# Two-layer graph block on one core: the row minimum of negated, scaled scores becomes the bias of the exponentials, with all engine orders rewritten

## The reference

```python
# layer 0
mi, mj = x @ Wi.T, x @ Wj.T
out = deg[None, :, None] * (mi + b) + einsum('ij,bjo->bio', a, mj)
x = layernorm(x + out)
# layer 1: 8 heads of 64
q, k, v = h @ Wq.T + bq, h @ Wk.T + bk, h @ Wv.T + bv
scores = einsum('bhqd,bhkd->bhqk', q, k) / sqrt(64)
scores = where(adj == 0, -inf, scores)
out = softmax(scores) @ v
x = layernorm(x + (out @ Wo.T + bo))
```

## Time and profile before

| | |
|---|---|
| Median of 3 runs | 3001.79 us (3000.93 to 3002.13) |
| The profiled execution's own time | 3026.84 us |
| Its span, first to last instruction | 3024.9 us |
| PE busy | 96% of the span |
| DVE busy | 79% |
| POOL busy | 62% |
| ACT busy | 62% |
| Share of the 16 DMA engines | 31% |
| Mean granted TensorE clock | 0.995 of full speed |

### The profile page before, as it was taken

The page is one execution under the profiler, slowest core; times in us unless marked ns, Lnnn a source line. Parts: engine busy times, 40 slices in busy tenths (PEclk is TensorE's granted clock), DMA queues, the critical chain, the costliest instruction groups (busy, mean ns, idle before and its releaser), DMA issues.

```text
span 3024.9 us, 59823 instructions
## 1 busy us (share of the span) xinstructions
PE 2903.7 (96%) x18584; PEld 2456.9 (81%) x18584; DVE 2377.9 (79%) x6029; ACT 1862.6 (62%) x4874; POOL 1877.5 (62%) x1793
## 2 busy tenths in 40 slices
PE   7999999999999999999999999999999999999997
PEld 5888888888788888888887888888888878878886
DVE  7787787877877878878778778787787787787876
ACT  4666656656666566666666665665666666656664
POOL 4666666666566666666665665666666666656563
PEclk9999999999999999999999999999999999999998
DMA  4333333333323333323333233332332332332321
GB/s 137 101 105 98 111 97 104 104 97 104 100 95 111 97 104 110 98 97 108 100 104 99 95 111 97 100 108 97 104 104 95 106 104 97 111 97 97 105 92 55
DMA packets 282404, 306.71 MB, mean 101 GB/s; under 512 B 18816, under 2 KB 214912, under 8 KB 282368
## 3 DMA queue, kind: packets, MB, share of 16 engines
q1 hardware_dynamic: 282368, 306.26, 31.2%
HBM read 173.55 MB, written 132.64 MB: 101 GB/s over the span
## 4 chain that ended last, share of the span: by engine, by line
PE 46%; DVE 24%; issue 16%; POOL 8%; ACT 5%; DVEq 1%; POOLq 0%; DMA 0%; SPq 0%; ACTq 0%
PE proj L493 25%; PE av L493 7%; PE proj L611 6%; DVE probs L1036 5%; PE attn L655 4%; ACT probs L820 4%; PE proj L530 3%; DVE oT L1087 3%; DVE exp_bias L1043 3%; DVE xb L1113 2%; POOL pT_lo L397 2%; DVE xb L1119 2%; PE attn L670 1%; DVE v_both L990 1%; POOL probs L388 1%
## 5 line engine op out<-in xcount | busy, mean ns | idle before, releaser
L820 ACT ACTIVATE probs<-probs,exp_bias 128x256 f32<-128x256 f32 x1024 | 508.6, 498 | 342.2 <-DVE exp_bias L1043 342.1
L388 POOL TENSOR_TENSOR probs<-probs,row_inv 128x512 f32<-128x512 f32 x256 | 266.5, 1041 | 476.6 <-DVE row_inv L1053 476.6
L1036 DVE CUSTOM_DVE_ANT_0 probs<-attn,mask_add 128x256 f32<-128x256 f32 x1024 | 381.1, 419 | 148.0 <-PE attn L655 147.7
L397 POOL TENSOR_TENSOR pT_lo<-pT_raw,pT_hi 128x512 fp32r<-128x512 f32 x315 | 402.9, 1296 | 149.2 <-ACT pT_hi L851 148.9
L530 PE MATMUL proj<-wji_hi,xs_hi 128*128 128x512 f32 x896 | 382.3, 427 | 24.7 <-DVE xb L1113 11.8
L530 PE MATMUL proj<-wji_hi,xs_lo 128*128 128x512 f32 x896 | 355.4, 397 | 0.0
L530 PE MATMUL proj<-wji_lo,xs_hi 128*128 128x512 f32 x896 | 355.3, 397 | 0.0
L611 PE MATMUL proj<-mj_hi,wq_hi 128*128 128x256 f32 x1024 | 293.5, 287 | 26.3 <-DVE mj_lo L990 26.3
L493 PE MATMUL av<-pT_hi,v_both 128*128 128x256 f32 x1016 | 266.1, 294 | 47.3 <-DVE oT L1087 29.1
L1144 DVE TENSOR_SCALAR hb<-hb,mean_var_out,rstd_out 128x512 f32<-128x512 f32 x128 | 122.3, 996 | 226.9 <-POOL rstd_out L415 226.9
L420 POOL TENSOR_TENSOR oT_lo<-oT,oT_hi 128x256 fp32r<-128x256 f32 x256 | 194.4, 759 | 151.7 <-ACT oT_hi L864 151.6
(11 more groups left out here) (125 smaller groups left out, 8824.5 us busy)
## 6 DMA issues: line engine op xcount, KB each, us to landing
bounce<-probs SPq DMA_DIRECT2D x189, 512.0 KB, 2.6
pT_raw<-bounce SPq DMA_DIRECT2D x756, 128.0 KB, 3.1
xs_raw<-in_xT SPq DMA_DIRECT2D x64, 512.0 KB, 4.1
xb<-in_x SPq DMA_DIRECT2D x64, 512.0 KB, 3.4
out<-hb SPq DMA_DIRECT2D x64, 512.0 KB, 2.8
w_raw<-in_w0T SPq DMA_DIRECT2D x8, 256.0 KB, 6.0
stage<-in_wqT SPq DMA_DIRECT2D x1, 1024.0 KB, 9.8
stage<-in_wkT SPq DMA_DIRECT2D x1, 1024.0 KB, 11.6
```

The costliest lines, as they stand in the source:

```text
L388: pool.tensor_tensor(e, e, inv, ALU.mult).then_inc(norm_odd_done, 1)
L397: pool.tensor_tensor(pT_lo[:, g % 2, :, :, i, :, :], pT_raw[:, g % 2, :, :, i, :, :], pT_hi[:, :, :, i, :, :].bitcast(F32), ALU.subtract). ...
L820: last = nc.scalar.activation(e, e, ACT.Exp, bias=exp_bias[:, g % 2, s:s + 1], scale=SCALE, accum_out=row_sum[:, g % 2, s:s + 1])
L1036: last = V.tensor_tensor_reduce(out=out_, in0=in_, in1=mask_, scale=1.0, scalar=MASKED, op0=ALU.add, op1=ALU.max, accum_out=row_max[:, g % ...
```

## The change

The weights and the bias of q are multiplied by -1/8 once, at the start: Wq's high part in ACT's copy, its raw values on POOL (half 0, in place, a new instruction with a wait behind it) and in DVE's subtraction (half 1), and `bq_cols` on DVE (128x4), for which ACT waits. So the scores come out negated and scaled. The mask is 0 or +3.0e38, the reduction is a minimum that starts from 1.0e37, and `row_min` is itself the bias: exp(row_min - e). `bias_of_pair`, `exp_bias` and `bias_done` are gone; the exponentials wait for the two minima of the pair. In `last_step` nothing else changes. In `step` the lists of POOL, PE, ACT and DVE are reordered; SP's is not.

```diff
-MASKED = -3.0e38
-MAX_FLOOR = -1.0e37
+MASKED = 3.0e38
+MIN_CEILING = 1.0e37
...
# POOL
             def sum_x(n):
+                pool.wait_ge(normed["h"], R * n)
                 pool.wait_ge(xT_loaded, 16 * (n + 1))
...
             pool.wait_ge(w_hi_done, 1)
+            pool.tensor_scalar(stage[0][:, 0:2, :], stage[0][:, 0:2, :], -SCALE, None, ALU.mult).then_inc(wq_scaled, 1)
+            pool.wait_ge(wq_scaled, 1)
...
                 n = b + 1
+                if y_: split_o(b - 1, 3)
                 normalise_odd(b, 1)
                 normalise_odd(b, 0)
-                if y_: split_o(b - 1, 3)
                 mj_low(n, 0)
                 mj_low(n, 1)
+                normalise_odd(b, 2)
                 root("h", n)
-                normalise_odd(b, 2)
-                if ahead: sum_x(b + 2)
                 p_low(b, 1, 0)
                 p_low(b, 1, 1)
                 normalise_odd(b, 3)
-                if ahead: add_bias(b + 2, parity)
-                split_o(b, 0)
+                if ahead: sum_x(b + 2)
                 p_low(b, 2, 0)
                 p_low(b, 2, 1)
+                if ahead: add_bias(b + 2, parity)
+                if y_: root("out", b - 1)
                 if ahead: x_low(b + 2, 0)
+                p_low(b, 3, 0)
+                if ahead: x_low(b + 2, 1)
+                split_o(b, 0)
                 split_o(b, 1)
-                if y_: root("out", b - 1)
-                p_low(b, 3, 0)
                 split_o(b, 2)
-                if ahead: x_low(b + 2, 1)
                 residual(n, 1 - parity, stored=y_)
...
# PE
                 attend(b, 0, not y_)
                 transpose_h(n, 0, 1 - parity)
+                scores(b, 1, only=3)
                 transpose_h(n, 1, 1 - parity)
-                scores(b, 1, only=3)
                 q(n, 0)
+                q(n, 1)
                 attend(b, 1)
-                q(n, 1)
                 k(n, 0)
                 k(n, 1)
+                v(n, 0)
                 attend(b, 2)
-                v(n, 0)
                 v(n, 1)
                 attend(b, 3)
...
# ACT
-                act.wait_ge(bias_done, G * b + at(g, tail) + 1)
+                act.wait_ge(max_done, 2 * (G * b + at(g, tail)) + 2)
...
-                        last = nc.scalar.activation(e, e, ACT.Exp, bias=exp_bias[:, g % 2, s:s + 1], scale=SCALE,
+                        last = nc.scalar.activation(e, e, ACT.Exp, bias=row_min[:, g % 2, s:s + 1], scale=-1.0,
...
                 if y_: v_high(b, 0)
+                if y_: o_low_part(b - 1, 3)
                 if y_: v_high(b, 1)
-                if y_: o_low_part(b - 1, 3)
                 mj_copy(n, U1)
                 exponentials(b, 1)
                 mj_copy(n, Z1)
                 mj_copy(n, U2)
+                if y_: o_high(b - 1, 3)
+                exponentials(b, 0)
                 normalise_even(b, 1)
-                exponentials(b, 0)
-                if y_: o_high(b - 1, 3)
+                mj_high(n, 0)
                 normalise_even(b, 0)
-                mj_high(n, 0)
                 mj_high(n, 1)
                 mj_high(n, 2)
                 pt_high(b, 0, 0, not y_)
+                exponentials(b, 2)
                 pt_high(b, 0, 1, not y_)
-                exponentials(b, 2)
                 normalise_even(b, 2)
+                o_low_part(b, 0, not y_)
                 hT_high(n, 0)
-                o_low_part(b, 0, not y_)
                 hT_high(n, 1)
                 p_high(b, 1)
                 exponentials(b, 3)
+                normalise_even(b, 3)
+                o_high(b, 0, not y_)
                 q_high(n, 0)
-                normalise_even(b, 3)
+                o_low_part(b, 1)
+                p_high(b, 2)
+                q_high(n, 1)
+                k_high(n, 0)
                 if ahead: x_high(b + 2, 0)
-                o_low_part(b, 1)
-                o_high(b, 0, not y_)
-                q_high(n, 1)
                 if ahead: x_high(b + 2, 1)
-                p_high(b, 2)
-                k_high(n, 0)
                 o_high(b, 1)
...
# DVE
                     last = V.tensor_tensor_reduce(
-                        out=out_, in0=in_, in1=mask_, scale=1.0, scalar=MASKED, op0=ALU.add, op1=ALU.max,
-                        accum_out=row_max[:, g % 2, s:s + 1])
+                        out=out_, in0=in_, in1=mask_, scale=1.0, scalar=MIN_CEILING, op0=ALU.add, op1=ALU.min,
+                        accum_out=row_min[:, g % 2, s:s + 1])
...
                 n, other = b + 1, 1 - parity
+                if y_: v_low(b, 0)
+                if y_: o_sum(b - 1, 3)
                 maxima_of_head(b, 1, 0, not y_)
-                if y_: v_low(b, 0)
                 maxima_of_head(b, 1, 1, not y_)
-                bias_of_pair(b, 1)
                 l0_sum(n, U1, other)
                 if y_: v_low(b, 1)
                 maxima_of_head(b, 0, 0, not y_)
                 maxima_of_head(b, 0, 1, not y_)
                 l0_sum(n, Z1, other)
+                l0_sum(n, U2, other)
                 inverse_sums(b, 1)
-                l0_sum(n, U2, other)
-                bias_of_pair(b, 0)
-                if y_: o_sum(b - 1, 3)
                 l0_sum(n, M2, other)
+                inverse_sums(b, 0)
                 l0_sum(n, U3, other)
-                inverse_sums(b, 0)
                 l0_sum(n, Z2, other)
                 flip(b, 1)
                 l0_sum(n, U4, other)
                 maxima_of_head(b, 2, 0)
                 maxima_of_head(b, 2, 1)
+                agg_sum(n, 0, other)
                 pt_low(b, 0, 0)
-                agg_sum(n, 0, other)
-                bias_of_pair(b, 2)
+                agg_sum(n, 1, other)
                 norm_stats("h", n, 0, read["agg"], h_row[other])
-                agg_sum(n, 1, other)
+                inverse_sums(b, 2)
                 norm_stats("h", n, 1, read["agg"], h_row[other])
                 norm_mean("h", n)
-                inverse_sums(b, 2)
                 pt_low(b, 0, 1)
...
                 hT_low(n, 0)
                 maxima_of_head(b, 3, 0)
                 hT_low(n, 1)
+                if y_: norm_stats("out", b - 1, 0, read["y"], hb_row[other])
                 maxima_of_head(b, 3, 1)
-                bias_of_pair(b, 3)
                 o_sum(b, 0, not y_)
                 inverse_sums(b, 3)
+                if y_: norm_stats("out", b - 1, 1, read["y"], hb_row[other])
+                flip(b, 3)
                 q_low(n, 0)
-                flip(b, 3)
-                if y_: norm_stats("out", b - 1, 0, read["y"], hb_row[other])
                 o_sum(b, 1)
-                if y_: norm_stats("out", b - 1, 1, read["y"], hb_row[other])
+                if y_: norm_mean("out", b - 1)
                 q_low(n, 1)
                 k_low_half(n, 0)
-                if y_: norm_mean("out", b - 1)
                 if y_: norm_apply("out", b - 1, hb_row[other])
                 o_sum(b, 2)
```

22 lines of the change are left out of this document (11 added, 11 removed).

## The result

The changed kernel takes 2930.0 us (median of 4 runs, 2927.8 to 2932.2), against 3001.4 us for the kernel before: a ratio of 0.976, with an interval of 0.975 to 0.9775, 71 us less. The profiled execution after took 2929.39 us with a span of 2927.6 us, as long as the plain runs; before, it was 25 us longer (3026.84 against 3001.79).

A forecast was written before the change was run, and what follows sets the result against it. PE (TensorE) was taken as the bound, with stalls to win. Terms 0.7 + 0.5 - 0.1 + 0.45 - 0.3 = 1.25 us per step, times 63, with the last step 80 us: 2921 us predicted, range 2888 to 2975.

The forecast's parts named there:

- exp_bias goes: Head of the step: exponentials wait for the minima themselves, all three first-layer stalls go, gain 0.7 of 0.8 us.
- h norm: DVE's norm of h, with POOL's sum_x moved away and POOL idle: the pair falls from 2.06 towards 1.1 us.
- q's start: PE order: pair 3's scores between the halves of hT give DVE 0.9 us of cover for half 0, gain 0.5.
- attend(b,1): PE order: q(n,1) goes ahead, covering p_low(b,1) and o_sum(b,0); gain 0.45 us, in a long step 1.55.
- The end of the step: Open term at attend(b,3): out norm blocked by POOL delays DVE; bounds gain 0.2 to loss 1.0, taken as loss 0.3.
- rival 1: Norm, o_sum, p_low(b,3,1) meet POOL's work; attend(b,3) stalls 0.8 to 1.2 us, time 2950 to 2980; chance 0.2.
- The start-up at changes of operand rows: PE: each change between 128-row transposes and 64-row scores costs about 0.1 us at the next matmul; minus 0.1.
- The queues: SP's order unchanged; flip(b,3) waits for the later attend(b,1), holding q_low(n,0) and o_sum(b,1); zero, with little cover.
- Rivals 2 and 3: 2: flip chain makes it slower, chance 0.05. 3: no gain, late q_low or hT_low, 2995 to 3008, chance 0.05.
- Prologue: POOL's added scaling of 128x1024 ahead of wq_lo fits its 2.71 us idle before root: zero, at worst 0.8 us more.
- Long steps: Held exp_bias delays o_sum(b,0), attend(b,1) waits; each costs 1.1 us, and plain runs have hardly any.
- rivals 1 and 4: 1: end of step swallows the gain, chance 0.2. 4: all stalls but a tenth go, 2895, chance 0.2.

The follow-up runs named there:

- min_only: The kernel before with the new arithmetic (no exp_bias) and all four engine orders as before: 2948.5 us, ratio 0.983.
- ht_early: The changed kernel with PE's hT half 0 ahead of attend(b,0), half 1 ahead of pair 3's scores, other engines following: 2910.8 us, ratio 0.969.
- attend1_back: The changed kernel with attend(b,1) back between the two halves of q on PE: 2984.1 us, ratio 0.995.
- sumx_early: The changed kernel with POOL's order altered: sum_x, add_bias and split_o(b,0) earlier, both x_low ahead of p_low(b,3,0): 2931.8 us, ratio 0.976.
- split_wait: The changed kernel with attend(b,3) waiting for POOL's half before its first head, DVE's half only before the second: 2898.2 us, ratio 0.966.
- orders_sumx: New orders with exp_bias kept, plus POOL's sum_x, add_bias, split_o(b,0) and both x_low moved earlier: 3000.8 us, ratio 1.000 against the kernel before.
- bias3_late: The kernel before with exp_bias of pair 3 moved behind o_sum(b,0): 3066.3 us, ratio 1.022.
- orders_only: The changed kernel with the old arithmetic, each exp_bias right behind its pair's second maximum: 3184.6 us, ratio 1.061 against the kernel before.

## Why the prediction was right, and where it was not

The time (2921 forecast, 2930 measured), the sign and the main mechanism were right: the stalls of PE were found one by one, and most of what they cost went. That no more than 9 us are missing is in part luck: the gain at q is about 0.2 us a step smaller than its terms say and the loss at the end of the step 0.15 larger, with another cause, while exp_bias brought 0.09 more than its term. Term by term, for a step:

- **exp_bias goes**: 0.7 predicted. The first layer fell from 10.69 to 9.90 us, 0.79; min_only isolates it at 0.82 a step. Right, and the most valuable term: 52 of the 71 us.
- **h norm**: from 2.06 us the pair to 1.00, near the 1.1 forecast; what it is worth by itself was not tried. In the lines view (`x128`, busy and mean of one) it stands as below, against 1058 ns before; the out norm went the other way, from 996 to 1258, and in this kernel it cost nothing.

```profile
L1145 DVE TENSOR_SCALAR xb<-xb,mean_var_h,rstd_h 128x512 f32<-128x512 f32 x128 | 64.2, 544 | 1.8 <-POOL rstd_h L418 1.8
...
L1145 DVE TENSOR_SCALAR hb<-hb,mean_var_out,rstd_out 128x512 f32<-128x512 f32 x128 | 156.0, 1258 | 188.1 <-POOL rstd_out L418 188.1
```

- **q's start**: gain 0.5 predicted, 0.25 measured (0.69 to 0.445). The term was mis-sized: the step said that 0.9 us of scores is cover enough for half 0 of hT. The chain behind it, ACT's copy and then DVE's mj_lo, is longer: PE's transposes of half 0 end at 1427.52, the copy lasts from 1427.73 (behind o_part) to 1428.32 and mj_lo to 1429.04. flip(b,2), ahead of mj_lo on DVE, ends at 1428.37. ht_early, which moves both, gave the other 0.24; which of its moves did it was not taken apart.
- **attend(b,1)**: 0.45 predicted and 0.46 measured against min_only (0.48 to 0.12 us, and the 0.10 of start-up). What I didn't see is that in the new order of the other engines the same place would cost 0.85 if PE had not moved (attend1_back).
- **The end of the step** was the step that failed: a loss of 0.3, with the out norm's block as its cause. The stall came, and its loss was 0.40 (0.41 to 0.805) against the mean of before; against a short step like that of the earlier trace rows it is 0.45. But the norm's block is hidden (sumx_early, where it doubles). The cause is p_low(b,3,1) of DVE, held by p_low(b,3,0) of POOL from 0.69 to 1.26 us, together with a wait that asks for both halves (split_wait). That is the part of rival 1 that names p_low(b,3,1), at a stall of 0.57 us instead of 0.8 to 1.2. The numbers of the earlier trace rows had pointed to it; I put the term's cause on the instruction that was already seen blocked, not on the one that would newly stand beside POOL's. The block that I named is real in orders_sumx, where the norm ends late enough; here POOL's p_low ends later than it.
- **The start-up at changes of operand rows** (0.1) is there: behind the scores of pair 3 the transposes start 0.21 and 0.16 us apart, instead of 0.12 and 0.11. With it, from the last matmul of attend(b,0) to the second of q it is 2.58 us instead of 2.80 in the two steps shown, 0.22 less, where 0.5 - 0.1 was predicted.
- **The queues** (flip, q_low): no wait of PE for them appears. Rivals 2 and 3 did not come. DVE's busy time fell to 34.8 us a step, not to about 33, as the out norm and p_low(b,3,1) became longer.
- **Prologue**: zero was right. The timeline of POOL:

```profile
32.30 2.78 POOL L439 TENSOR_SCALAR stage<-stage 128x1024 f32<-128x1024 f32 x1
35.16 2.35 POOL L441 TENSOR_TENSOR wq_lo<-stage,wq_hi 128x1024 fp32r<-128x1024 f32 x1
37.46 0.19 POOL L415 TENSOR_TENSOR var_eps_h<-mean_var_h,eps_cols 128x2 f32<-128x2 f32 x1
```

  Scaling and wq_lo end where root starts: the 2.71 us of idle time of the earlier trace rows is used up, and no more. The first scores behind the prologue start at 61.7 us, where they started at 61.6.
- **Last step**: 1 us predicted, not shown. It took 45.3 us at a granted clock of 0.90, but the kernel before took 47.7 at 0.80 and 45.9 at 0.86 in two executions, and sumx_early and split_wait, with the changed last step, took 48.4 and 48.8 at 0.77.
- **Long steps**: the reading that plain runs have few of them fits the times, but no plain run was traced. The cause, a held exp_bias, holds; the route through o_sum is one of two (bias3_late).
- **The chances**: the forecast and rivals 1 and 4 alone make 0.9, so the 0.9 for "faster" leaves no room for the piece of rival 3 that the text adds.

Sum of the step: 1.25 predicted, 1.10 measured.

The Trainium skill (SBUF — State Buffer, Who interferes with whom) says that a DVE instruction with two inputs in SBUF contends with a GpSimd one that reads SBUF; this trace agrees, with 0.69 us alone and 1.26 beside p_low(b,3,0). The Trainium skill (GPSIMD Engine Reference, Instruction dispatch) puts about 6 us on the first call to a freshly loaded kernel; no row here shows such a cost: the first scaling took 2.78 us, and the step behind the prologue starts 0.1 us later than before.

What the change's two halves do to each other was not in the prediction: alone, the arithmetic is worth 1.7% and the orders cost 6.1%; together they are worth 2.4%. The new orders have no slack for a late exp_bias, and are only good without it. What exactly decides whether a given step of the kernel before is long stays open. In all 37 long steps of the two profiled executions exp_bias of pair 3 starts within 0.02 us of POOL's second p_low, but so it does in most short ones (27.08 to 27.14 us into the step, in long and short ones alike). The steps in which it starts 0.05 us or more ahead are all short.

## What to carry to other kernels

- An instruction of 128x4 elements can cost a microsecond when it falls beside GpSimd's work: look at the largest and the median of its time, and not only at the smallest.
- Before two instructions are put side by side on two engines, ask which waits stand over both; let the consumer wait for each half where it uses it. Here that moved nothing and gave 32 us.
- The same stall at the same instruction can have another cause in a neighbouring order (the norm in orders_sumx, p_low in the changed kernel): look at which of two ends comes last.
- A new order is to be judged with the lateness that its queues can take. Read each stall by the distance between starts in one step, and change one thing at a time: a stall that is removed by an earlier start of something else can come back at another place.

## What the runs showed of the hardware that was not expected

- DVE's TENSOR_TENSOR with both inputs in SBUF, 128x512, took 0.69 us alone, 1.26 beside POOL's p_low (1.29 us) and 1.83 beside a POOL x_low of 2.52 us (orders_only); it ended 0.55 us behind p_low(b,3,0). POOL's side varies too: an x_low of 128x1024 takes 2.83 us in the changed kernel, 2.52 in orders_only, and wq_lo of that size 2.35; which DVE instruction does that was not taken apart.
- DVE's norm pair (128x512, two instructions) took 1.00 us with POOL idle, 2.51 beside one x_low of 128x768 and 4.58 beside both x_low. It ended 0.74 and 0.28 us behind the POOL instructions beside it (1.84 and 4.37 us), so it followed their length more than its own work.
- The reduction with min takes 419 ns in the mean (128x256, x1024), and the one with max took 419.
- In orders_only a stall of 3.15 us stood in each step, and in 34 of 62 steps it was followed by matmuls at half speed, with a granted clock of 0.963 over the execution; starts 1.38 us behind in every step of orders_sumx were not (0.994).
- Two profiled executions of one kernel had last steps of 47.7 and 45.9 us, at granted clocks of 0.80 and 0.86.
